# Cross-attention with an 8-bit feed-forward on one core: the first batch's products of context and weights ahead of its first scores, loads by turns

## The reference, cut to what matters

```python
# x, ctx: (8, 512, 512) f32; mask: (8, 512, 512), 1.43 or 0, one pattern per batch
def block(x, ctx, mask, W, b, wq, wscale, ffn_bias):
    q = layernorm(x)                                    # eps 1e-5
    scores = einsum('bqd,bkd->bqk', q, ctx) / 0.72
    attn = softmax(scores, axis=-1) * mask
    x = x + einsum('bqk,bkd->bqd', attn, ctx) @ W + b @ W
    y = layernorm(x)
    s = max(max|y| over a row, 1e-6) / 127              # rows to 8 bits
    return x + (round(y / s) @ wq.T) * s * wscale + ffn_bias
```

## Time and profile before

| what | value |
|---|---|
| three runs | 315.61, 315.90, 321.22 us, median 315.9 |
| profiled execution | 315.67 us, of which 313.9 us are the span from first to last instruction |
| PE busy | 305.4 us of the span (97%), 1395 matmuls |
| POOL, DVE, ACT busy | 265.5 (85%), 258.9 (82%), 245.9 us (78%) |
| granted TensorE clock, mean | 0.995 |
| first matmul, first product that the reference needs (first scores) | 0.97 us, 8.60 us |

### The profile page before, as it was taken

The page is one execution under the profiler, slowest core; times in us unless marked ns, Lnnn a source line. Parts: engine busy times, 40 slices in busy tenths (PEclk is TensorE's granted clock), DMA queues, the critical chain, the costliest instruction groups (busy, mean ns, idle before and its releaser), DMA issues.

```text
span 313.9 us, 5314 instructions
## 1 busy us (share of the span) xinstructions
PE 305.4 (97%) x1395; PEld 241.6 (77%) x1410; DVE 258.9 (82%) x565; ACT 245.9 (78%) x500; POOL 265.5 (85%) x363
## 2 busy tenths in 40 slices
PE   8999999999999999999999999999999999999983
PEld 8988878777777877777778777777877777787771
DVE  1997784899888888988888898888889888779785
ACT  4466875898988878898888889888888888777651
POOL 3285667899999989999999999999999999969783
PEclk9999999999999999999999999999999999999998
DMA  7995968799996999999999989888976986442303
GB/s 202 275 257 165 199 190 238 224 243 248 278 246 198 261 275 269 220 264 274 227 270 236 271 214 245 260 253 245 262 253 174 260 240 198 143 139 63 69 33 134
DMA packets 88173, 68.39 MB, mean 218 GB/s; under 512 B 25040, under 2 KB 67792, under 8 KB 88144
## 3 DMA queue, kind: packets, MB, share of 16 engines
q1 hardware_dynamic: 80368, 53.90, 65.9%
q10 hardware_dynamic: 7776, 14.16, 14.9%
HBM read 41.16 MB, written 22.54 MB: 203 GB/s over the span
## 4 chain that ended last, share of the span: by engine, by line
PE 96%; DVE 1%; issue 1%; ACT 0%; DVEq 0%; POOL 0%; POOLq 0%
PE ps_scores L651 9%; PE ps_scores L653 9%; PE ps_scores L652 9%; PE ps_attn L652 9%; PE ps_attn L653 9%; PE ps_attn L651 9%; PE ps_ffn L821 8%; PE ps_vw L653 5%; PE ps_vw L651 5%; PE ps_vw L652 5%; PE ps_ut L651 4%; PE ps_ut L653 4%; PE ps_ut L652 4%; PE ps_ffn L639 1%; PE ps_pt L643 1%; PE ps_scores L661 1%
## 5 line engine op out<-in xcount | busy, mean ns | idle before, releaser
L651 PE MATMUL ps_scores<-ct_hi,xt_hi 128*128 128x512 f32 x124 | 48.5, 391 | 0.0
L653 PE MATMUL ps_scores<-ct_hi,xt_lo 128*128 128x512 f32 x124 | 48.3, 389 | 0.0
L652 PE MATMUL ps_scores<-ct_lo,xt_hi 128*128 128x512 f32 x124 | 48.2, 389 | 0.0
L651 PE MATMUL ps_attn<-vw_hi,pt_hi 128*128 128x512 f32 x120 | 46.8, 390 | 0.0
L653 PE MATMUL ps_attn<-vw_hi,pt_lo 128*128 128x512 f32 x120 | 46.7, 389 | 0.0
L652 PE MATMUL ps_attn<-vw_lo,pt_hi 128*128 128x512 f32 x120 | 46.7, 389 | 0.0
L1561 POOL TENSOR_TENSOR x_in<-x_in,bias_w 128x512 f32<-128x512 f32 x32 | 41.2, 1286 | 0.7 <-issue 0.7
L1534 POOL TENSOR_TENSOR ct_lo<-ct_raw,ct_hi 128x512 fp32r<-128x512 f32 x28 | 36.7, 1311 | 3.6 <-ACT ct_hi L889 3.6
L1542 POOL TENSOR_TENSOR xt_lo<-xt_raw,xt_hi 128x512 fp32r<-128x512 f32 x29 | 37.7, 1299 | 0.8 <-ACT xt_hi L924 0.7
L1591 POOL TENSOR_TENSOR x_plus<-x,ffn_bias_wide 128x512 f32<-128x512 f32 x27 | 35.0, 1296 | 3.6
L1251 DVE TENSOR_REDUCE neg_max<-ps_scores 128x1 f32<-128x512 f32 x32 | 22.0, 688 | 17.5 <-PE ps_scores L653 17.4
(11 more groups left out here) (189 smaller groups left out, 833.1 us busy)
## 6 DMA issues: line engine op xcount, KB each, us to landing
x_in<-in_x_dram SPq DMA_DIRECT2D x32, 256.0 KB, 3.2
mask_in<-in_mask_BxSxS_fk_dram SPq DMA_DIRECT2D x32, 256.0 KB, 3.7
norm_rows<-x_norm ACTq DMA_DIRECT2D x30, 256.0 KB, 3.4
x_blocks<-norm_rows SPq DMA_DIRECT2D x120, 64.0 KB, 2.8
out_dram<-out_tile SPq DMA_DIRECT2D x30, 256.0 KB, 3.7
ctx_in<-in_ctx_dram SPq DMA_DIRECT2D x56, 128.0 KB, 3.7
prob_rows<-probs ACTq DMA_DIRECT2D x24, 256.0 KB, 3.1
wq_rows<-prob_rows SPq DMA_DIRECT2D x96, 64.0 KB, 3.2
```

The costliest lines, as they stand in the source:

```text
L651: nc.tensor.matmul(bank_, lhs_hi(t), rhs_hi(t), start=(t == 0), stop=False)
L652: nc.tensor.matmul(bank_, lhs_hi(t), rhs_lo(t), start=False, stop=False)
L653: last = nc.tensor.matmul(bank_, lhs_lo(t), rhs_hi(t), start=False, stop=(t == NT - 1))
```

## The change

It touches only the prologue and step 0. SP loads context and W by turns, and row tile 0 behind them. PE turns two context tiles, then makes the twelve matmuls of each vw in groups of three by arrival of the chunk of W and of the context tile (accumulating in four banks at once), turns row tile 0 between them, and comes to the first scores only behind all four vw. The first scores are then an ordinary step's 12 matmuls of 512 columns. ACT and DVE split in the new order of arrival. In step 0, ACT has row tile 2's normalisation, its store, the high part of context 4 and vw 0 and 1 ahead of the exponentials, DVE has vw 0 and 1 ahead of the row maximum, and POOL's cast of the 8-bit weights comes behind the low part of context 4. Three warm-up products between transposes and two of the seven ahead of them are gone; context tiles share two banks.

```diff
-WARM_UPS = 7
-
-BETWEEN = 3
+WARM_UPS = 5
-        first_ct_banks = [ps_ct, ps_vw, ps_pt, ps_attn]
+        first_ct_banks = [ps_ct, ps_pt, ps_ct, ps_pt]
 # SP
-            load_x(0, 0)
-            for t in range(PER_BATCH):
-                sp.dma_start(ctx_in[:, t, :], ctx_flat[t * P:(t + 1) * P, :]).then_inc(first_ctx_loaded[t], 16)
-            for t in range(NT):
-                sp.dma_start(w_raw[:, t, :], weights.rearrange("(p t) e -> p t e", t=NT)[:, t, :]) \
-                    .then_inc(w_loaded[t], 16)
+            for t in range(PER_BATCH - 1):
+                load_first_ctx(t)
+                load_w(t)
+            load_w(NT - 1)
+            load_first_ctx(PER_BATCH - 1)
+            load_x(0, 0)
 # PE
-            def first_scores():
...
+            def turn_first_ctx(t):
+
+                if t >= 2:
+                    pe.wait_ge(ct_lo_ready, t - 1)
+                pe.wait_ge(first_ctx_loaded[t], 16)
+                for i in range(NT):
+                    last = nc.tensor.transpose(first_ct_banks[t][:, i * P:(i + 1) * P],
+                                               ctx_in[:, t, :].rearrange("p (c t) -> p t c", t=NT)[:, i, :],
+                                               identity[:, :])
+                last.then_inc(first_ct_done, 1)
+
+            def first_ctx_times_w(j, t):
+
+                into = first_vw_banks[j][:, :]
+                whole, low = ct_hi[:, 0, t, j * P:(j + 1) * P], ct_lo[:, 0, t, j * P:(j + 1) * P]
+                pe.wait_ge(ct_hi_ready, j + 1)
+                pe.wait_ge(w_hi_ready, t + 1)
+                nc.tensor.matmul(into, whole, w_hi[:, t, :], start=(t == 0), stop=False)
+                pe.wait_ge(ct_lo_ready, j + 1)
+                nc.tensor.matmul(into, low, w_hi[:, t, :], start=False, stop=False)
+                pe.wait_ge(w_lo_ready, t + 1)
+                last = nc.tensor.matmul(into, whole, w_lo[:, t, :], start=False, stop=(t == NT - 1))
+                if t == NT - 1:
+                    last.then_inc(vw_done, 1)
...
+            turn_first_ctx(0)
+            turn_first_ctx(1)
+            first_ctx_times_w(0, 0)
+            first_ctx_times_w(1, 0)
+            turn_first_ctx(2)
+            for j in range(2):
+                first_ctx_times_w(j, 1)
+            for t in range(2):
+                first_ctx_times_w(2, t)
+            turn_first_ctx(3)
+            for t in range(2, NT):
+                for j in range(3):
+                    first_ctx_times_w(j, t)
+            turn_row_tile(0, first_xt_done)
+            for t in range(NT):
+                first_ctx_times_w(3, t)
 # PE, step 0 behind the scores
-                        ctx_times_w(base, d + 2, first_vw_banks[2])
-
                         turn_row_tile(1, first_xt_done)
-                        ctx_times_w(base, d + 3, first_vw_banks[3])
+                        next_vw(d + 4)
                         turn_probs(d)
                         add_bias_terms()
 # ACT, prologue
+            for t in range(2):
+                split_first_ctx(t)
+                split_w(t)
+            split_w(2)
+            split_first_ctx(2)
+            split_w(3)
+            split_first_ctx(3)
+            normalise(HEAD, PER_BATCH)
             normalise(HEAD, PER_BATCH + 1)
+            act.wait_ge(first_xt_done, 1)
+            split_x(PER_BATCH, ps_xt[:, :])
 # ACT, step 0
+                    normalise(base, d + 2)
+                    store_rows(base, d + 2, (base + d + 2) * P)
                     split_next_ctx(d + 4)
+                    for t in range(2):
+                        split_vw(base, d + t, first_vw_banks[t])
...
-                    normalise(base, d + 2)
-                    store_rows(base, d + 2, (base + d + 2) * P)
-                    for t in range(2):
-                        split_vw(base, d + t, first_vw_banks[t])
                     act.wait_ge(first_xt_done, 2)
                     split_x(d + 1, ps_xt[:, :])
 # DVE, prologue
+            for t in range(2):
+                split_first_ctx(t)
+                split_w(t)
+            split_w(2)
+            split_first_ctx(2)
+            split_w(3)
             x_statistics(HEAD, PER_BATCH)
             x_mean_var(PER_BATCH)
+            split_first_ctx(3)
             x_statistics(HEAD, PER_BATCH + 1)
             x_mean_var(PER_BATCH + 1)
...
+            split_x(HEAD, PER_BATCH, ps_xt[:, :])
             x_statistics(HEAD, PER_BATCH + 2)
             x_mean_var(PER_BATCH + 2)
 # DVE, step 0, ahead of the row maximum, and behind bias_terms_lo
                     turn_ctx(base, d + 4)
+                    for t in range(2):
+                        split_vw(base, d + t, first_vw_banks[t])
...
-                    for t in range(2):
-                        split_vw(base, d + t, first_vw_banks[t])
                     turn_ctx(base, d + 5)
                     split_x(base, d + 1, ps_xt[:, :])
 # POOL, from the prologue into step 0
                     split_next_ctx(d + 4)
+                    pool.wait_ge(wq_loaded, 16)
+                    nc.gpsimd.tensor_copy(flat(wq_rows[:, :, :]), flat(wq_words[:, :, :]).bitcast(I8)) \
+                        .then_inc(wq_rows_ready, 1)
```

More of the change, by code:

```diff
@@ L644, in transpose4, with product3 @@
                 last.then_inc(done, 1)
-            def product3(bank_, lhs_hi, lhs_lo, rhs_hi, rhs_lo, done, before=None):
+            def product3(bank_, lhs_hi, lhs_lo, rhs_hi, rhs_lo, done):
                 for t in range(NT):
-                    if before:
-                        before(t)
                     nc.tensor.matmul(bank_, lhs_hi(t), rhs_hi(t), start=(t == 0), stop=False)
@@ L680, in ctx_times_w @@
                          lambda t: ct_lo[:, half, t, j * P:(j + 1) * P],
-                         lambda t: w_hi[:, t, :], lambda t: w_lo[:, t, :], vw_done,
-                         before=(lambda t: pe.wait_ge(w_lo_ready, t + 1)) if is_tile(base, n, 0) else None)
+                         lambda t: w_hi[:, t, :], lambda t: w_lo[:, t, :], vw_done)
             def add_bias_terms():
@@ L706, in _ @@
             pe.wait_ge(identity_ready, 1)
[L707 to L717, removed]
-            def step(base, d):
-                if is_tile(base, d, 0):
-                    first_scores()
-                    for t in range(2):
-                        ctx_times_w(base, d + t, first_vw_banks[t])
-                elif exists(base, d):
+            turn_first_ctx(0)
[14 more added lines that the diff above has]
+                first_ctx_times_w(3, t)
+            def step(base, d):
+                if exists(base, d):
                     k = slot(d, 2)
@@ L868, in step @@
                 else:
[L869 to L872, removed]
                     if is_tile(base, d, 0):
-                        ctx_times_w(base, d + 2, first_vw_banks[2])
                         turn_row_tile(1, first_xt_done)
-                        ctx_times_w(base, d + 3, first_vw_banks[3])
+                        next_vw(d + 4)
                         turn_probs(d)
                         add_bias_terms()
-                    next_vw(d + 4)
+                    else:
+                        attend(d - 1)
+                        turn_probs(d)
+                        next_vw(d + 4)
             run_steps(pe, step)
@@ L934, in _, with split_first_ctx, split_w @@
             nc.scalar.activation(ones_r[:, :], ones[:, :], ACT.Copy).then_inc(ones_r_ready, 1)
[L935 to L940, removed]
+            def split_first_ctx(t):
                 act.wait_ge(first_ct_done, t + 1)
                 split_ctx(PER_BATCH + t, first_ct_banks[t][:, :].rearrange("p (t k) -> p t k", t=NT))
-            for t in range(NT):
+            def split_w(t):
                 act.wait_ge(w_loaded[t], 16)
                 nc.scalar.activation(w_hi[:, t, :], w_raw[:, t, :], ACT.Copy).then_inc(w_hi_ready, 1)
+            for t in range(2):
[6 more added lines that the diff above has]
+            normalise(HEAD, PER_BATCH)
             normalise(HEAD, PER_BATCH + 1)
+            act.wait_ge(first_xt_done, 1)
+            split_x(PER_BATCH, ps_xt[:, :])
             act.wait_ge(bias_terms_ready, NT)
@@ L1184, in x_mean_var, with split_w @@
                 nc.vector.bn_aggr(meanvar1[:, slot(n, 4), :], stats1[:, slot(n, 4), :]).then_inc(meanvar1_ready, 1)
+            def split_w(t):
+                dve.wait_ge(w_hi_ready, t + 1)
+                lo_part(w_lo[:, t, :], w_raw[:, t, :], w_hi[:, t, :], w_lo_ready)
+            for t in range(2):
[4 more added lines that the diff above has]
+            split_w(3)
             x_statistics(HEAD, PER_BATCH)
             x_mean_var(PER_BATCH)
-            for t in range(PER_BATCH):
-                if t == PER_BATCH // 2:
-                    split_x(HEAD, PER_BATCH, ps_xt[:, :])
-                split_first_ctx(t)
-            for i in range(NT):
-                dve.wait_ge(w_hi_ready, i + 1)
```

(5 more changed lines are left out.)

2 lines of the change are left out of this document (added).

## The result

The changed kernel takes 322.01 us (five runs, 321.0 to 322.26) against 315.9 for the kernel before (five runs, four of them 315.1 to 316.38): the ratio is 1.019, 95% interval 1.0167 to 1.0213. The fifth run of the kernel before, 321.22, was in a slower state of the chip and is not in the ratio. It is slower by 1.9%, where 1.4% was forecast (320.4) and 316.6 to 322.2 was the range; the time lies 0.2 us inside its upper end. The profiled execution took 322.01 with a span of 320.2, 6.3 over the span before.

A forecast was written before the change was run, and what follows sets the result against it. PE, with 96% of the chain, was taken as the bound. Late row tiles and the second wait delay step 1's scores by 3.8 us, its transposes by 4.7 in all: 315.67 + 4.7 = 320.4 us, range 316.6 to 322.2.

The forecast's parts named there:

- PE's start: Prologue: first vw product at 6.7 us, 2.1 earlier, but transposes and waits between groups eat the gain.
- unknown costs: Landings of turns, tile 1's factors and PE's pace: landings taken as 0, factors at 2.7 us, pace rising near 7.1.
- rival C: Loads: W's strided rows land slowly, c1 and all behind 1.1 us later; 321.5, with rival B 322.4; chance 0.09.
- rival B: PE's start: the clock rises later because of the new gap, forecast plus 0.9, 321.3 us; chance 0.13.
- The late row tiles: Step 0: tile 2's normalisation and store precede context 4's split on ACT, so PE waits 2.1 us before vw 4.
- The second wait: Behind vw 4: DVE's late row maximum and splits delay step 1's scores by 3.8 us, its probabilities' transposes by 4.7 in all.
- The idle PE ahead of step 1's scores: Sign of being right: PE idle there, waiting for DVE's low part of row tile 1; scores start near 30.7.
- Rival A: Row tiles' path: DVE and ACT keep ahead, not slower, 315.3 to 316.0 us; half of it 317 to 318.5; chance 0.2.
- Rival D: First vw groups: they don't get ahead, as products wait for each other's splits; partly in the sum, no chance given.
- Small parts: Prologue and step 0: changed warm-up products, POOL's moved cast, shared context banks and four open banks cost 0.

The follow-up runs named there:

- e1: Changed kernel with row tile 2's statistics moved ahead of row tile 0's low part on DVE; 319.83 us, 1.0088 against the kernel before.
- e4: Changed kernel with eight more warm-up products on PE ahead of vw 4 in step 0; 321.62 us, 1.015 against the kernel before.
- e2: Changed kernel with high parts of context 4, vw 0 and 1 ahead of row tile 2's normalisation and store on ACT; 320.44 us.
- f2: Changed kernel with the edits of e1, e2 and e3 together; 318.29 us, 1.0091 against the kernel before.
- e5: Changed kernel with each chunk of W loaded as 128 neighbouring rows instead of every fourth row; 321.86 us, one run.
- f3: As f2, with context 5's transpose, bias low part and tile 3's statistics before DVE's row maximum, row tile 1's split before the mask; 319.12 us.
- f6: As f3, but the bias terms' low part stays behind the mask and row tile 3's statistics precede tile 0's low part on DVE; 319.2 us.
- f1: The changed kernel unaltered, run again beside f2, f3 and f5; 321.73 us, 1.0188 against the kernel before.
- f4: Changed kernel with DVE made to wait for row tile 1's norm factors ahead of the bias terms; 321.97 us, one run.
- f5: Changed kernel with row tile 0 loaded ahead of the turns of context and W loads; 322.93 us, 1.0221 against the kernel before.
- e6: Changed kernel with the four context tiles loaded ahead of the four chunks of W, row tile 0 still last; 323.49 us, one run.
- e3: Changed kernel with four more warm-up products between the transposes of the first and second context tile; 320.68 us, 1.0129 against the kernel before.

## Why the prediction was right

**PE's start.** Forecast: first vw product at 6.7, c3 turned by 12.6. Measured 7.91 and 14.6 (in the chain's counting, as the forecast was). Two of the unknown costs, both taken at nothing, fell on the bad side together: the second context tile landed at 6.7 instead of 5.7 (rival C, its size of 1.1 about right, its cause, W's strided rows, not shown), and the pace doubled at 10.5 instead of 7.1 (rival B, 0.9; its cause, the gap, not shown). e1's profile had both on the good side, and its T is 12.03 (forecast 12.1); e4's had the late tile and the early pace, with 12.81; the changed kernel had both on the bad side, with 13.94. Forecast plus both was 322.4 in the prediction; measured is 322.0. The start is 2.0 late and the path behind it 0.4 shorter than forecast, which makes the 1.6 us by which 320.4 was short. The prediction named both costs and the pair, but the side on which they fell it had wrong, and this range had 0.2 us left for it: that the time lies inside is in part luck.

**The late row tiles.** From c3's transposes to those of step 1's probabilities the forecast had 24.9 us (12.1 to 37.0), and the chain has 24.5 (14.10 to 38.56). Its links held one by one: POOL's factors of tile 1 2.7 (2.70), the wait of PE ahead of vw 4 2.1 (2.0), the move of context 4's high part behind tile 2's store (0.4 for its issue). e1 and e2 cut this path and got about 2 us of it each, and f2 showed that it is in the main one path.

**The second wait.** DVE's row maximum of step 1 was forecast 1.1 behind the end of the scores and is (35.2, 36.3), and the chain does run through DVE from `pt_lo` to `probs`; PE's visible wait is 0.5, for the attention product covers the rest. The idle PE ahead of step 1's scores, which the prediction named as a sign that it was right, is not there in the changed kernel. By the prediction's own numbers this wait for row tile 1's low part was 1.7 us (29.0 to 30.7); it shows as 0.8 in e1 to e5. What I did not see is why it is missing: PE was slow there, since the clock fell behind the 2 us wait, and its own list filled the time. That cost 0.2 by the pair of the changed kernel and e5; without a later wait the same fall would cost 1.5, by an estimate from the start of step 0's probabilities in that pair (30.04, 31.58).

**Rival A**, not slower: its point of decision, tile 2's factors by 18.5, was missed by 5 us (23.84), and e1 shows that this was what decided, for it makes them ready 2 us earlier, counted from T, and gets 2 us. **Rival D** was in the sum as far as it came true: the 18 products ahead of T and c2's transposes took 6.2 us (7.91 to 14.10) where 5.4 were forecast, and the slow pace was forecast to cost about that difference.

**Small parts.** The moved cast, the shared banks and the four open accumulations cost nothing that shows: vw groups go on at 0.23 each across banks, from 14.32 to 18.54.

## What to carry to other kernels

When work of the bound engine is moved to an earlier place, ask what now arrives last and which single instruction of it stands in front of an unrelated one on another engine: here the normalisation of a later row tile, in ACT's list ahead of a context tile, held PE for 2 us, while the early products brought no earlier end in any run. From f3 and f6: an instruction moved into an idle gap is free only if its data has landed by then and its neighbour on the other engine does not share its ports. And two unknown costs that each look small should be weighed as a pair when a likeliest number and a range are chosen: here they came together.

## What the runs showed of the hardware

- The granted-clock row says 1.00 for every microsecond of the start, in both kernels. Yet in the changed kernel matmuls of one shape start 0.43 apart ahead of 10.5 us and 0.23 after, and in the kernel before the same four transposes take 1.10 at 4.31 and 0.64 at 7.72. Later in the changed kernel's trace the row says 0.50 to 0.52 where matmuls are 0.43 apart, and in f3 it says 0.50 at the start too, from 8 to 11 us. So at the start a row of 1.00 can be wrong, and the pace is the evidence.
- Seven profiles have the 2 us wait ahead of vw 4. The granted clock over 24 to 32 us was 0.79 in the changed kernel, f1, f4 and f5, 0.86 in e6, and 1.00 in e3 and e5: the same wait leads to a fall in one execution and not in another.
- The fall made vw 4 take 4.4 us instead of 2.9 and moved U by 0.2 (38.34 in e5, 38.56 in the changed kernel): where PE would have waited 0.8 us anyway, most of a slow stretch does not reach the end.
- Of two instructions on DVE and POOL with SBUF operands side by side, either can pay: DVE 1.70 instead of 0.67, POOL 2.70 instead of 1.36 for its four.
